# A new hand-written order of the last group and of its rest, without the clock-keeping matmuls, in a fused perceiver layer

## What is computed

```python
xn = norm(norm0(x)) * g1 + be1
q, k, v = xn @ Wq, split(ctx @ Wkv)                 # 16 heads of 64, 257 context rows
x = x + softmax(where(mask, q k^T / 8, -inf)) v @ Wo + bo
xn = norm(norm0(x)) * g2 + be2
q, k, v = split(xn @ W_qkv + b_qkv)                 # 16 heads of 16, 32 tokens
x = x + softmax(q k^T / 4) v @ W_proj + b_proj
x = norm0(x);  x_prev = x shifted by one token, per sequence
r = sigmoid((mur * x + (1 - mur) * x_prev) @ W_r)
k = (muk * x + (1 - muk) * x_prev) @ W_k
out = x_before_norm0 + r * (relu(k)^2 @ W_v)
```

## Time and profile before

| | us |
|---|---|
| median of three runs | 845.15 (844.27 to 845.73) |
| the profiled execution | 844.62 |
| its span, first to last instruction | 842.7 |
| busy in the span: PE | 799.9 (95%) |
| busy: ACT, DVE, POOL | 604.0, 600.3, 415.0 |

### The profile page before, as it was taken

One profiled execution on the slowest core, in us unless ns is written; L12 is line 12 of the kernel. 1 busy time (PEld: TensorE's weight loads), 2 busy tenths in 40 slices (PEclk: granted clock), 3 DMA queues, 4 the chain that ended last, 5 costly groups with the idle time before them and its releaser, 6 DMA issues.

```text
span 842.7 us, 20502 instructions
## 1 busy us (share of the span) xinstructions
PE 799.9 (95%) x7501; PEld 665.1 (79%) x7501; DVE 600.3 (71%) x1813; ACT 604.0 (72%) x1439; POOL 415.0 (49%) x664
## 2 busy tenths in 40 slices
PE   9999899999999999998999999999999989888885
PEld 8988688876889678895888768896788957777664
DVE  5865857786687956788577866879568783767375
ACT  3998767796678956887678966789568875677422
POOL 1356345663456624763456624566247633475311
PEclk9999999999999999999999999999999999999999
DMA  9311110110101200011101101012000110100000
GB/s 238 131 40 38 50 26 14 39 58 8 30 11 39 63 23 17 16 33 56 26 14 39 48 17 27 14 39 63 17 24 14 29 48 14 26 14 1 27 2 14
DMA packets 49523, 30.53 MB, mean 36 GB/s; under 512 B 22928, under 2 KB 48336, under 8 KB 49424
## 3 DMA queue, kind: packets, MB, share of 16 engines
q1 hardware_dynamic: 48528, 29.12, 12.7%
q10 hardware_dynamic: 896, 0.10, 0.1%
HBM read 26.85 MB, written 2.10 MB: 34 GB/s over the span
## 4 chain that ended last, share of the span: by engine, by line
PE 78%; DVE 14%; ACT 3%; issue 3%; POOL 1%; POOLq 0%; ACTq 0%; DVEq 0%
PE score L807 17%; PE probT L818 6%; PE post L895 6%; PE pre L657 6%; DVE qk_t L1356 4%; DVE qk_l L1352 3%; PE post L904 3%; PE aux L746 3%; PE ac_main L835 3%; PE ac_tail L837 3%; PE ac_main L836 3%; PE ac_tail L841 3%; PE ac_main L840 2%; PE post L875 2%; PE post L881 2%
## 5 line engine op out<-in xcount | busy, mean ns | idle before, releaser
L431 POOL TENSOR_TENSOR prT_l<-prT,prT_h 128x512 fp32r<-128x512 f32 x128 | 166.0, 1298 | 197.3 <-ACT prT_h L1128 196.7
L565 POOL TENSOR_SCALAR pr<-pr,rsum,poison 128x257 f32<-128x257 f32 x256 | 146.3, 582 | 131.2 <-DVE rsum L1380 131.1
L1109 ACT ACTIVATE pr<-sm,nmx 128x257 f32<-128x257 f32 x256 | 129.6, 507 | 62.1 <-DVE nmx L1374 61.1
L1374 DVE CUSTOM_DVE_ANT_0 sm<-score,mbias 128x257 f32<-128x257 f32 x256 | 106.8, 420 | 80.3 <-PE score L807 65.5
L807 PE MATMUL score<-cT_h,qk_h 128*128 128x258 f32 x256 | 90.0, 351 | 6.7 <-DVE qk_t L1356 5.0
L1128 ACT ACTIVATE prT_h<-prT 128x512 fp32r<-128x512 f32 x128 | 80.6, 631 | 20.0 <-PE ac_tail L841 18.7
L818 PE MATMUL probT<-ident,pr 128*128 128x128 f32 x512 | 79.2, 277 | 0.7 <-ACT prT L1117 0.7
L1117 ACT ACTIVATE prT<-probT 128x512 f32<-128x512 f32 x128 | 75.6, 591 | 2.9 <-PE probT L818 1.7
L807 PE MATMUL score<-cT_h,qk_t 128*128 128x258 f32 x256 | 72.8, 284 | 0.0
L1387 DVE TENSOR_TENSOR act_<-ac_tail,act_low 64x256 f32<-64x256 f32 x128 | 52.8, 412 | 28.1 <-ACT act_low L1141 26.8
L807 PE MATMUL score<-cT_h,qk_l 128*128 128x258 f32 x256 | 72.5, 283 | 0.0
(11 more groups left out here) (319 smaller groups left out, 2181.5 us busy)
## 6 DMA issues: line engine op xcount, KB each, us to landing
cx_in<-in_ctx_dram SPq DMA_DIRECT2D x64, 192.0 KB, 2.5
cx_in<-in_ctx_dram SPq DMA_DIRECT2D x64, 64.0 KB, 2.3
xn<-in_x_dram SPq DMA_DIRECT2D x8, 256.0 KB, 3.0
xb<-in_x_dram SPq DMA_DIRECT2D x8, 256.0 KB, 3.0
out_dram<-yo SPq DMA_DIRECT2D x7, 256.0 KB, 2.2
wq<-in_L_xattn_Wq_dram SPq DMA_DIRECT2D x2, 512.0 KB, 6.0
wo<-in_L_xattn_Wo_dram SPq DMA_DIRECT2D x1, 1024.0 KB, 8.0
wqkv<-in_L_attn_W_qkv_dram SPq DMA_DIRECT2D x1, 768.0 KB, 8.9
```

Source lines behind the costliest of these rows:

```text
L431: eng.tensor_tensor(prT_l[:, :, cut], prT[:, :, cut], prT_h[:, :, cut], ALU.subtract).then_inc(prob_lower, 1)
L565: last = pool.tensor_scalar(p, p, rsum[:, j % 2, t:t + 1], poison[:, 0:1], ALU.mult, ALU.mult)
L1109: act.activation(pr[j % 2][:, t, :], sm[:, t % 2, :], ACT.Exp, bias=nmx[:, j % 2, t:t + 1], scale=-1.0, accum_out=ssum[:, j % 2, t:t + 1]) ...
L1374: dve.tensor_tensor_reduce(sm[:, t % 2, :], score[t % 2][:, 0:NK], mbias[:], DH ** -0.5, BIG, ALU.add, ALU.min, nmx[:, j % 2, t:t + 1]).th ...
```

## The change

Only the tables `PE_LAST`, `ACT_LAST`, `DVE_LAST` and `POOL_LAST` are replaced, and the jobs `Z` no longer occur in `PE_LAST`. The tables hold the same jobs otherwise. Groups 0 to 6 are untouched. One line of each kind of the diff, cut:

```diff
@@ PE_LAST
-    "FR FK P1:6 LT.0 FV S3:7 AC:6 P0:7 OT0.0 OT1.0 P1:7 LT.1 WO.0 AC:7 OT0.1 T2.0 OT1.1 QT.0 KT.0 WO.1 Z0 SC.0 VR.0 Z1 Z2 "
+    "S2:7 FK AC:5 S3:7 P1:6 FV P0:7 AC:6 OT0.0 P1:7 LT.1 OT1.0 AC:7 WO.0 OT0.1 OT1.1 WO.1 T2.0 QT.0 KT.0 T2.1 QT.1 KT.1 "
...
-FILL = tuple(f"Z{n}" for n in range(19))
+FILL = tuple(f"Z{n}" for n in range(17))
```

More of the change, by code:

```diff
@@ L73 @@
 PE_LAST = (
[5 rows of a table removed]
-    "T3.0 Z17 T3.1 FR.0 FK.0 FR.1 FK.1 Z18 FV.0 FV.1").split()
[4 rows of a table added]
+    "SC.0 VR.0 SC.1 VR.1 PT.0 PV.0 T4.0 PT.1 PJ.0 PV.1 T4.1 PJ.1 T3.0 T3.1 FR.0 FK.0 FR.1 FK.1 FV.0 FV.1").split()
 ACT_FIRST = (
@@ L92 @@
 ACT_LAST = (
[5 rows of a table removed]
-    "T4.1 T3.0 M0.0 T3.1 M0.1 FK.0 EZ.0 FK.1 EZ.1").split()
[5 rows of a table added]
+    "T3.0 M0.0 T3.1 M0.1 FK.0 EZ.0 FK.1 EZ.1").split()
 DVE_FIRST = (
@@ L111 @@
 DVE_LAST = (
[6 rows of a table removed]
-    "C8.0 PJ.1 C0.1 C1.1 C2.1 C9.0 C3.1 C4.1 C5.1 C6.1 C7.1 C8.1 C9.1 M1.0 M1.1 FR.0 FR.1 SG.0 FV.0 SG.1 FV.1").split()
[6 rows of a table added]
+    "C8.0 C9.0 PJ.1 C0.1 C1.1 C2.1 C3.1 C4.1 C5.1 C6.1 C7.1 C8.1 C9.1 M1.0 M1.1 FR.0 FR.1 SG.0 SG.1 FV.0 FV.1").split()
 POOL_FIRST = (
@@ L125 @@
 POOL_LAST = (
-    "N0:0 CT:1 N1:0 CT:2 XB L0:0 N0:1 CT:3 L1:0 CT:4 L0:1 N1:1 N0:2 L1:1 N1:2 X1 CT:5 N0:3 L0:2 N1:3 W0 L1:2 W1 L0:3 N0:4 "
-    "CT:6 N1:4 LX L1:3 N0:5 CT:7 N1:5 L0:4 L1:4 N0:6 L0:5 L1:5 N1:6 KA L0:6 L1:6 N0:7 YO N1:7 L0:7 CT:0 L1:7 XB.0 X1.0 "
+    "CT:1 XB N0:0 CT:2 N1:0 L0:0 LX N0:1 N1:1 CT:3 L1:0 N0:2 CT:4 N1:2 L0:1 L1:1 X1 CT:5 N0:3 L0:2 L1:2 N1:3 CT:6 W0 W1 "
+    "L0:3 N0:4 N1:4 CT:7 L1:3 N0:5 N1:5 L0:4 L1:4 N0:6 N1:6 L0:5 L1:5 CT:0 KA N0:7 L0:6 L1:6 N1:7 YO L0:7 L1:7 XB.0 X1.0 "
     "X1.1 W.0 W.1 KA.0 KA.1 YO.0 YO.1").split()
```

## The result

| | before | after |
|---|---|---|
| median, us | 845.01 (4 runs, 844.27 to 845.73) | 836.6 (4 runs, 835.63 to 837.92) |
| the profiled execution | 844.62 | 837.92 |
| its span | 842.7 | 836.1 |
| T, the start of `AC:7` | 790.34 | 777.26 |
| T to the second scaling `W.1` | 30.7 | 33.1 |

The changed kernel is faster: ratio 0.9902, 95% interval 0.9883 to 0.992. The forecast was 838.3. In the three stretches the profiled executions differ by -13.1, +2.3 and +4.1 us, which is the -6.6 of the span. The forecast had -9.4, +2.6 and nothing for the third: the sum came out well by luck, because two misses, 3.7 us too little gained ahead of T and 4.1 us lost behind `W.1`, nearly cancelled. The profiled execution is the slowest of the four.

The account below looks back on a forecast made before the run. Group 7 bound by PE's work plus 10.3 us of pauses, the rest by round trips between engines. 844.62 - 9.4 + 2.6 = 837.8, median 0.5 above: 838.3; forecast case 836.0 to 840.8, ends 835.5 and 843.8.

Parts of the forecast that it names:

- the prediction's own signs: T near 781, group 7 pauses 4 to 5 us, clock 1.00; wrong if T passes 785 or T-to-end 56 us.
- the place of the gain: Group 7 up to T: the new order brings T 9.4 us earlier, with FK, FV and OT1.0 covered.
- WO.0: On PE, moved from ahead of AC:7 to behind it: T falls by 3.6 us.
- the rest up to W.1: From T on: KM.1 at T + 22.15, W.1 at T + 33.3, 2.6 us later than before.
- the pauses in group 7: PE's pauses in group 7 fall from 10.3 to 4.5 us, a gain of 5.8.
- my allowance: 1.3 us added to 3.2 us of laid-out group 7 pauses for forgotten handoffs; without it the gain is 7.1.
- I take the full clock: In the rest: the clock outlives the longest expected pause, 3.75 us from VR.1 to PT.0.
- zero for the Z jobs: In the rest: removing the 19 identity jobs changes nothing, within 0 and -1.0 us.
- rival (a): Clock falls at the pause before PT.0, PE at 1.2 GHz to the end: +4.2 us, 842.5; chance 0.18.
- the small terms behind W.1: Three terms behind W.1: PJ.0 ahead of PV.1 +0.15, M1.0 0.35 sooner, YO.1 behind YO.0 +0.15 us.
- (b): Group 7's pauses only move and all 10.3 us stay: 844.1 us; chance 0.16.
- (c): DVE's queue in batches 4 and 5 runs late, making the kernel slower: 848.3 at 10 us late; chance 0.10.

Follow-up runs that it names:

- the crossed kernels: Two kernels: changed group order with before's rest and its identity matmuls, 834.15 us; before's group order with the changed rest and no identity matmuls, 847.59 us.
- the kernel with its own order: Changed kernel with PE's and DVE's order of the rest changed again and 15 identity jobs put in its pauses; 830.34 us, ratio 0.9827.
- the fitted kernel: Changed kernel with 17 identity jobs put into the pauses of its new rest, sized at 0.45 us each; 833.08 us, ratio 0.9856.
- the kernel with one pause filled: Changed kernel with seven identity jobs in one place alone, the pause between VR.1 and PT.0; 835.96 us, ratio 0.9883.

## Why the prediction was right, and where it was not

The time lies in the forecast's range, 836.6 against 838.3, but the prediction's own signs were not all met. T came at 777.3 where it had said near 781, PE paused for 1.4 us in group 7 and not 4 to 5, and the clock did not hold. It had also said that it would be wrong if more than 56 us passed from T to the end of the span: 58.8 did.

**Right: the place of the gain.** The group's order carries it, as the crossed kernels show. `FK`, `FV` and `OT1.0` no longer wait. That the named cover is the cause was shown for `FK`, whose pause came back without it (0.78 us); for the other two it was not tested.

**Right: WO.0.** Putting it back moved T by 3.85 us (forecast 3.6), and 1.7 of them are given back at `OT0.1` (forecast 1.95).

**Right: the rest up to W.1.** `KM.1` came at T + 22.2 (forecast 22.15), `W.1` at T + 33.1 (33.3). The chain of DVE's groups in the earlier trace rows gave 11.15 us from `KM.1` to `W.1`, measured 10.9, and a loss from T on of 2.6, measured 2.3. But this loss is no verdict on the new order of the rest. Most of it is `WO.0`, which now stands behind T: with it ahead of `AC:7` the new rest reaches `W.1` at T + 31.2 or 31.4, and with it behind the old rest does at T + 33.8. The kernel with its own order showed that the order of the rest still had 2.8 us to give.

**Mis-sized: the pauses in group 7.** The step was 10.3 down to 4.5, of which 3.2 were laid out and 1.3 my allowance. Measured are 1.4. Of the pauses that I had laid out by name, none came at `P0:3` and `T4`, 0.19 at `S2:5` and 0.53 at `S3:5`; the only other one is 0.30 at `T3`. Even the end that I kept without the allowance was too dear. The rest of the miss is PE's work itself. In the profiled execution of after the context transpose at the start of group 7 comes 0.6 us later than before (687.84 against 687.26), and from it to T are 89.4 us against 103.1. Of these 13.7 us 3.6 are `WO.0` and 8.9 the pauses; the other 1.2 are shorter work, which the prediction had said no order changes. Why the layout was too dear was not tested and stays open; the waits that remain are DVE's, 0.7 us for masks and 0.3 for a normalisation.

**Wrong: "I take the full clock", and zero for the Z jobs.** This is rival (a), which had 0.18: the clock fell 2.4 us into the pause that the prediction named (803.9 to 807.24), 3.33 us long. The price was well worked out (4.2; measured 4.5 in the profiled executions, 3.5 by the medians), the choice was wrong. The argument was a single row: that the clock fell 4.9 us after the last matmul, so that a pause of 3.75 would be outlived. That row shows one fall, and it bounds nothing: in after's own trace the last matmul ends at 831.0 and the clock falls at 833.6, 2.6 us later. In the kernel before without its Z jobs the clock fell after no pause longer than 2.6. By the page of the Trainium skill that was cited (TensorE: Matmul & The Clock Gate, section on what's actually happening) the throttled state is the default and activity releases it. It was the better guide, and the traces agree with it: with the Z jobs 1.00 to the last matmul, without them 0.50 for 10 to 24 us in all, in each of three pairs (before, the fitted kernel and the one with its own rest, each against itself without the jobs). The other half of the argument, that their matmuls stood "in pauses" and so cost nothing, was right where it can be read at full clock: `T2.1` starts at T + 18.7 with them and at T + 18.6 without, in the kernel before. It was just not what they were there for.

**Right: the small terms behind W.1.** At full clock `W.1` to the end is 21.3 in the fitted kernel and 21.6 before, -0.35 where the three terms had -0.05.

**Not come: (b) and (c).** The pauses didn't move, and DVE's queue in batches 4 and 5 kept PE waiting for 0.7 us in all.

**Luck: the sum.** With the measured steps it reads 844.62 - 13.1 + 2.3 + 4.1 = 837.9, the profiled execution; the median of the four is 836.6. The forecast met it because the pauses gave more than forecast and the clock took about as much back. Where the clock was held, in the fitted kernel, the time is 833.08, below the forecast's 836.0 to 840.8.

## What to carry to other kernels

Matmuls that compute nothing may be there for the clock. Before they are taken out, look at how busy PE is over the whole stretch around them and not only at the longest pause, and price the pieces of PE work on the chain at the lower clock. In a chain of round trips through one queue it can pay to put two jobs with different partners next to each other: each covers the other's trip, and moving one uncovers both. This was shown at one place, `FR` and `P0:6`, in one execution. And where a change does two things at once, here a new order and the loss of the fillers, compare like with like: together they made a rest that loses, and what lost was the missing fillers, not the order.

If such fillers are used, fit them to the pause by what one takes in the trace: 34 of them held the clock and lost 2.7 us against 17.

## What the runs showed of the hardware

The clock can fall, rise and fall again within 20 us of thin work: down at 811.6, up at 815.1, down at 818.5, up at 825.3 in the kernel with one pause filled. How long it is down differs between executions (the mean granted clock of the four of the kernel with its own rest and no Z jobs is 0.984 to 0.994), and so do the times: the kernels in which it falls spread by 2.2 to 3.4 us over their runs, those in which it stays up by 0.7 to 1.6.

At the launch the pace of PE's first matmuls differs from run to run, with nothing of it in the granted clock, which reads 1.00 there. The same 36 matmuls at the start, in after and in the kernel with its own rest, and one stretch of each:

```profile
1.53 7.13 PE L992 MATMUL score<-ident 128*128 128x128 f32 x36 [1.53 <-POOL ident L531]
```

```profile
1.52 5.62 PE L994 MATMUL score<-ident 128*128 128x128 f32 x36 [1.52 <-POOL ident L533]
```

```profile
6.00:7.00 1.00, 1.00 (x6) 1.00 (x6) 0.90 (x5) 0.86 (x2) 0.00 (x0) 1.00 0.96 269
```

```profile
6.00:7.00 1.00, 1.00 (x11) 0.95 (x9) 0.89 (x6) 0.95 (x2) 0.00 (x0) 1.00 0.93 273
```

Six matmuls in a us against eleven. The eight kernels with the same order up to `AC:7` had 5.62 to 7.13 us for this row and T from 776.06 to 777.26, in nearly the same sequence. So up to some 1.2 us of any difference between two single executions of this kernel can come from its first 9 us; the stretches from T on, by which the experiments are read, don't carry it.
